# Moving the norm, the transposes, the logits and the choice of experts of seven token groups between the shared experts' slots

## The chip, the cores and the metric

The kernel runs as one program on one core of a Trainium2 chip. The metric is the device time of one launch in microseconds; the kernel before takes 1272.83 us, the median of three runs (1271.46 to 1273.12).

## The reference

The input is 8 x 512 tokens of 256 numbers, fp32. Three layers are applied in a row, each on a layer norm of the current x: half a mixture-of-experts layer, an attention layer with landmark tokens and an iterated pseudo-inverse, and the mixture-of-experts layer again with the same weights.

```python
def _L0_ffn_ref(hidden_states, gate_w, shared_gate, shared_up, shared_down, r_gate, r_up, r_down):
    x = hidden_states.reshape(-1, h)
    shared_out = _swiglu(x, shared_gate, shared_up, shared_down)      # silu(x @ wg.T) * (x @ wu.T) @ wd.T
    logits = x @ gate_w.T                                             # 8 experts
    top_id = jnp.argmax(logits, axis=-1)
    score = jax.nn.sigmoid(jnp.max(logits, axis=-1))
    xs = x * score[:, None]
    ... # for each expert e: routed += _swiglu(xs where top_id == e else 0, r_gate[e], r_up[e], r_down[e])
    return (shared_out + routed_out).reshape(b, s, h)

x = x + 0.5 * _L0_ffn_ref(_layernorm(x), ...)
x = x + _L0_attn_ref(_layernorm(x), ...)
x = x + 0.5 * _L0_ffn_ref(_layernorm(x), ...)
```

Every token goes to one expert only, and its row is scaled by the score before the expert's gate and up products.

## The kernel before

Everything is hand-scheduled: each engine (TensorE = PE, VectorE = DVE, ScalarE = ACT, GpSimd = POOL, SyncE = SP for DMAs) has one list of instructions that it works off in order, and semaphores make it wait for others. The 4096 tokens are 32 tiles of 128 rows, in 8 groups of 4 tiles. X stays in SBUF. A mixture-of-experts layer (the code calls it FFN, n = 0 and n = 1) has three stages.

The front stage, for every group g: DVE takes mean and variance (`bn_stats`, `bn_aggr`), ACT the square root (L897), DVE the reciprocal and the normalised rows (L364), PE transposes them with 8 matmuls against the identity (L1336), ACT copies the result from PSUM into XNT (L912). After groups 0 to 4 and again at the end PE makes the logits (L1363), ACT copies them (L916), PE turns them back (L1372), and DVE chooses the expert of every token (L452 to L460). Only then does PE start on the shared expert.

The shared expert is computed in 32 slots, slot = 4g + f, f being the quarter of the 512 hidden columns. In a slot PE does gate and up (L1403, 12 matmuls of 512 columns: a product of fp32 numbers is made from three products of their high and low parts), ACT the silu (L950), DVE the product h (L533), ACT its high part hh (L956), DVE its low part hl (L535), and PE the down product two slots later (L1416, 12 matmuls of 256 columns). Once in a group DVE adds the result onto X (`shared_out`, L527), ACT and DVE split the next group's transposed tokens (L935, L432). Beside it, in group 0, DVE counts the tokens of each expert and works out each token's slot in a table sorted by expert. POOL multiplies each row by norm and score (L1176 to L1182), SP stores it to `xs_dram` (L298), and POOL scatters the token numbers to `who_dram` (L1189), 4 tiles at a time. In slots 28 to 31 the first expert weights are split as well (ACT L966, DVE L557). They overwrite groups 0 to 5 of X, so ACT waits until these are stored (L305).

The routed stage has 39 tiles of the table. POOL gathers a tile's rows (L1202) and residual rows (L1208) and scatters the outcome (L1214); PE transposes the rows (`xt`, L1435), does gate and up (`through`, L1446), turns the hidden rows (L1453) and does down (L1460); ACT and DVE split rows and weights. For the first tile `xt` comes after all of the shared experts' work.

The attention stage between the two layers runs over periods, in which the steps of several batches are interleaved; the last period has only the output projection of the last batch left (`project`, L1682).

## Time and profile before

| what | us |
|---|---|
| median of three runs (lowest, highest) | 1272.83 (1271.46, 1273.12) |
| span of the profiled execution | 1266.7 |
| PE busy / DVE / ACT / POOL | 1143.0 / 768.9 / 601.1 / 582.6 |
| chain that ended last, PE's share | 73% |
| stage, FFN 0: until the first shared matmul | 0 to 44.4 |
| shared slots | 44.4 to 184.35 |
| routed tiles | 187 to about 398 |
| attention | about 400 to 887 |
| stage, FFN 1: front after attention | 887 to 912.7 |
| shared slots | 912.7 to 1051.4 |
| routed tiles | 1054 to 1266 |

No time of the profiled execution is given other than its span; the median lies 6.1 us above the span (start and end of the launch). PE is busy in nearly all of the shared and routed stages, and in the stages between them it is not.

### The profile page before, as it was taken

To read this page: it belongs to the slowest core of one execution; us is meant where nothing else is said; L and a number is where in the kernel's file an instruction comes from. 1 tells how busy PE (TensorE), PEld (TensorE's weight loads), DVE (VectorE), ACT (ScalarE), POOL (GpSimd) and SP (SyncE) were. 2 spreads that over 40 slices of the span, in tenths; PEclk is the share of its full clock that TensorE was granted. 3 is DMA by queue.
4 is the path that set the end of the run, shared out by engine and by line. 5 is a ranking of instruction groups with operands and counts; after the bars stand their busy time and mean duration, and the time that the engine had idled before them with its cause. 6 is when DMAs were issued, how large, how long until landed. Compare 5 with 4: busy or idle time off the path is not lost.

```text
span 1266.7 us, 29890 instructions
## 1 busy us (share of the span) xinstructions
PE 1143.0 (90%) x11140; PEld 933.2 (74%) x11141; DVE 768.9 (61%) x1467; ACT 601.1 (47%) x968; POOL 582.6 (46%) x624
## 2 busy tenths in 40 slices
PE   4899999999995689898898998986799998999997
PEld 2688877888884567667676776864588887888886
DVE  7554456666663574656757657652664455676664
ACT  2533336666663445445454543431533344666663
POOL 0388505767775121432423232232058713677675
PEclk9899999999997889999999999997799999999999
DMA  8311542222211200000000000000611343222220
GB/s 331 151 34 50 184 144 74 69 69 72 62 57 53 84 2 3 2 2 3 2 3 2 2 3 2 3 2 1 267 35 50 99 147 118 64 66 63 69 71 21
DMA packets 41964, 80.32 MB, mean 63 GB/s; under 512 B 8948, under 2 KB 33655, under 8 KB 40832
## 3 DMA queue, kind: packets, MB, share of 16 engines
q1 hardware_dynamic: 28576, 53.54, 11.7%
q0 software_dynamic: 13280, 25.24, 6.6%
q8 instruction: 80, 1.31, 0.4%
q14 instruction: 28, 0.23, 0.1%
HBM read 57.17 MB, written 27.07 MB: 67 GB/s over the span
## 4 chain that ended last, share of the span: by engine, by line
PE 73%; DVE 14%; ACT 6%; issue 5%; DMA 1%; POOL 0%; DVEq 0%; ACTq 0%; POOLq 0%
PE PS L1446 17%; PE PS L1403 11%; PE PS L1460 10%; PE PS L1416 6%; PE PS L1644 3%; PE PS L1631 3%; PE PS L1522 3%; PE PS L1453 3%; DVE A_NM L669 2%; PE PS L1682 2%; DVE A_NM L676 1%; PE PS L1532 1%; PE PS L1591 1%; PE PS L1435 1%; PE PS L1665 1%
## 5 line engine op out<-in xcount | busy, mean ns | idle before, releaser
L1446 PE MATMUL PS<-WHL,XGH 128*128 128x512 f32 x624 | 218.9, 432 | 8.2 <-DVE XGL L580 4.5
L1272 POOL TENSOR_TENSOR A_A<-A_XC,A_ST 128x320 f32<-128x320 f32 (+1 forms) x96 | 74.3, 789 | 193.5 <-ACT A_ST L1053 193.4
L1460 PE MATMUL PS<-WD,XNT 128*128 x624 | 148.4, 381 | 1.5 <-ACT XNT L989 1.5
L1202 POOL DMA_INDIRECT X<-xs_dram,WHO x78 | 117.7, 1508 | 48.8 <-issue 48.8
L587 DVE TENSOR_TENSOR XNT<-XNT,PS 128x512 f32<-128x512 f32 x78 | 53.6, 688 | 133.3 <-PE PS L1446 133.3
L1446 PEld LDWEIGHTS PS<-WHL,XGH 128*128 128x128 f32 x624 | 113.0, 192 | 28.2 <-DVE XGL L580 5.0
L1446 PE MATMUL PS<-WHL,XGL 128*128 128x512 f32 x312 | 124.5, 399 | 0.0
L1460 PEld LDWEIGHTS PS<-WD,XNT 128*128 128x128 f32 x624 | 112.5, 190 | 14.4 <-issue 2.0
L985 ACT ACTIVATE XNT<-PS 128x512 f32<-128x512 f32 x78 | 46.6, 598 | 150.4 <-PE PS L1446 150.4
L1208 POOL DMA_INDIRECT HSB<-shared_dram,WHO x78 | 80.2, 1028 | 79.6 <-DMA shared_dram<-X 56.4
L1416 PE MATMUL PS<-SDH,HHL 128*128 128x256 f32 x512 | 103.0, 285 | 2.3 <-DVE X L527 1.8
L557 DVE TENSOR_TENSOR WHL<-WG,WHL 128x1024 fp32r<-128x1024 f32 x78 | 94.7, 1215 | 2.6 <-ACT WHL L966 2.6
L557 DVE TENSOR_TENSOR WHL<-WU,WHL 128x1024 fp32r<-128x1024 f32 x78 | 95.1, 1219 | 0.0
L1416 PEld LDWEIGHTS PS<-SDH,HHL 128*128 128x128 f32 x512 | 83.7, 191 | 10.0 <-issue 7.7
L950 ACT ACTIVATE HSB<-PS 128x512 f32<-128x512 f32 x64 | 38.2, 597 | 107.3 <-PE PS L1403 106.8
L533 DVE TENSOR_TENSOR HSB<-HSB,PS 128x512 f32<-128x512 f32 x64 | 44.0, 688 | 64.8 <-ACT HSB L950 64.7
L1403 PE MATMUL PS<-XHL,SGH 128*128 128x512 f32 x256 | 82.0, 402 | 1.2 <-DVE XHL L432 1.2
L535 DVE TENSOR_TENSOR HHL<-HSB,HHL 128x512 fp32r<-128x512 f32 x64 | 48.4, 756 | 56.7 <-ACT HHL L956 56.7
L966 ACT CAST WHL<-WU 128x1024 fp32r x78 | 82.7, 1060 | 0.0
L966 ACT CAST WHL<-WG 128x1024 fp32r x78 | 81.8, 1048 | 1.7 <-issue 1.7
L1189 POOL DMA_INDIRECT who_dram<-STOK,SIDX x64 | 69.9, 1092 | 27.5 <-issue 14.3
L757 DVE SCALAR_TENSOR_TENSOR A_BU<-PS,A_XC 128x320 f32<-128x320 f32 (+1 forms) x96 | 41.1, 443 | 65.1 <-PE PS L1631 59.5
(240 smaller groups left out, 2700.4 us busy)
## 6 DMA issues: line engine op xcount, KB each, us to landing
WG<-in_r_gate SPq DMA_DIRECT2D x2, 4096.0 KB, 15.9
WU<-in_r_up SPq DMA_DIRECT2D x2, 4096.0 KB, 17.4
xs_dram<-X SPq DMA_DIRECT2D x16, 512.0 KB, 2.9
WD<-in_r_down SPq DMA_DIRECT2D x4, 2048.0 KB, 8.3
shared_dram<-X SPq DMA_DIRECT2D x16, 512.0 KB, 8.3
X<-in_x SPq DMA_DIRECT2D x4, 1024.0 KB, 9.0
X<-mid_dram SPq DMA_DIRECT2D x8, 512.0 KB, 3.8
X<-xs_dram,WHO POOLq DMA_INDIRECT x78, 3.6
```

What stands on the lines that cost most here:

```text
L535: dve.tensor_tensor(B["HHL"][2 * (f % 2) + 1][:], hidden, B["HHL"][2 * (f % 2)][:].bitcast(F32), ALU.subtract).then_inc(s["hl"], 1)
L557: dve.tensor_tensor(WHL[2 * slot + 1][:], B[w][:, bass.ds(ex * (KD * F), KD * F)], WHL[2 * slot][:].bitcast(F32), ALU.subtract).then_inc(s ...
L587: dve.tensor_tensor(B["RH"][:, u * F:(u + 1) * F], B["RS"][:, u * F:(u + 1) * F], banks[3 + u][:], ALU.mult).then_inc(s["rh"], 1)
L966: act.copy(WHL[2 * slot][:], B[w][:, bass.ds(ex * (KD * F), KD * F)]).then_inc(s["whi"], 1)
L1189: pool.indirect_dma_start(out=who_dram[n], out_offset=bass.IndirectOffsetOnAxis(ap=B["SIDX"][:, j:j + 1], axis=0), in_=B["STOK"][:, j:j + ...
L1202: pool.indirect_dma_start(out=B["XS"][:, u * D:(u + 1) * D], out_offset=None, in_=xs_dram, in_offset=bass.IndirectOffsetOnAxis(ap=B["WHO"] ...
L1208: pool.indirect_dma_start(out=B["RY"][:, u * D:(u + 1) * D], out_offset=None, in_=shared_dram, in_offset=bass.IndirectOffsetOnAxis(ap=B["W ...
L1272: pool.tensor_tensor(a, x, st, ALU.add).then_inc(att["a"], 1)
L1403: ins = pe.matmul(banks[bank][:], w[:, part], tok[:, k * GW:(k + 1) * GW], start=(k == 0 and i == 0), stop=(k == KD - 1 and i == 2))
L1416: ins = pe.matmul(to, h[:, j * P:(j + 1) * P], w[:, part], start=(f == 0 and i == 0 and j % 2 == 0), stop=(f == KF - 1 and i == 2), skip_g ...
L1446: ins = pe.matmul(banks[bank][:], tok, w[:, k * F:(k + 1) * F], start=(k == 0 and i == 0), stop=(k == KD - 1 and i == 2))
L1460: ins = pe.matmul(banks[7][:, 0:D], B["HT"][:, u * F + f * P:u * F + (f + 1) * P], B["WD"][:, bass.ds(ex * (KF * D) + f * D, D)], start=(f ...
```

## The change

The front stage is cut down to group 0. Groups 1 to 7 have their norm on POOL (`rows`, into WG's buffer that the routed weights fill later), their transposes on PE behind the gate and up product of slots 1, 2, 3, 6, 7, 8 and 9 (`TURN_SLOT`), and their copies on ACT. Logits come in slots 4 and 10, are turned in slot 11, the choice follows in slot 11 on DVE, and the counting and the slot table in slots 13 to 15. The square roots are done in four lots in FFN 0 and in two in FFN 1. Group 0's high and low token parts are taken straight from PSUM.

For FFN 1, group 0's square root, normalised rows, transposes and split stand in the last period of the attention stage.

The input loads are by group, with the shared weights between them. Rows are stored to `xs_dram` normalised but without the score. The score is written beside the token number into the slot table (8 bytes for each slot instead of 4), comes back with it, and is applied in the routed stage: as `scale` of ACT's silu, and as a factor of DVE's product of silu and up. The 32 scatters to `who_dram` are issued in one go after slot 14.

At the seam to the routed stage, `xt` of tile 0 stands in slot 31 and of tile 1 ahead of tile 0's gate product, the last two down products lie between tile 0's gate and up products, and in all routed tiles `xt` and the gather run one tile further ahead.

```diff
+    DEVIATIONS = [[(0, 1), (1, 2), (2, 4), (4, NG)], [(0, NG - 1), (NG - 1, NG)]]
+    TURN_SLOT = {1: 1, 2: 2, 3: 3, 4: 6, 5: 7, 6: 8, 7: 9}
+    LOGIT_SLOTS = (4, 10)
+    TURN_LOGITS_SLOT = 11
+    COUNT_SLOT = 13
...
@@ SP, loads
+        load_x(0)
+        sp.dma_start(CB[:], consts).then_inc(s_const, 16)
+        sp.dma_start(SG, sh_gate).then_inc(s_shared[0], 16)
+        load_x(1)
+        sp.dma_start(SU, sh_up).then_inc(s_shared[1], 16)
...
@@ SP, in ffn_dma
-            with sp.Fori(0, NG) as g:
-                need(sp, "xs", g * GT + GT)
-                sp.dma_start(xs_rows[:, bass.ds(g * GT, GT), :], B["XS"].rearrange("p (t d) -> p t d", d=D)).then_inc(s["xs_out"], 16)
+            for g in range(1, NG):
+                store_rows(g)
...
             need(sp, "who", 16 * NT)
             sp.dma_start(B["WHO"][:], who_dram[n].rearrange("(p t) o -> p (t o)", p=P)).then_inc(s["who_sb"], 16)
+            for g in range(PARTS_G - 1, NG - 1):
+                store(g)
@@ DVE
+                    if n == 0 and slot == 1:
+                        rstd(n, 2)
+                    if n == 0 and slot < NG - 3:
+                        dve.wait_ge(s_x[slot + 3], 16)
+                        stats(slot + 3, n)
+                    if slot == TURN_LOGITS_SLOT:
+                        choose()
+                    elif slot == COUNT_SLOT:
+                        count_tokens()
+                    elif slot == COUNT_SLOT + 1:
+                        count_tiles()
+                        find_slots()
...
-                dve.tensor_tensor(B["RH"][:, u * F:(u + 1) * F], B["RS"][:, u * F:(u + 1) * F], banks[3 + u][:],
-                                  ALU.mult).then_inc(s["rh"], 1)
+                dve.scalar_tensor_tensor(B["RH"][:, u * F:(u + 1) * F], banks[3 + u][:], score(t), B["RS"][:, u * F:(u + 1) * F],
+                                         ALU.mult, ALU.mult).then_inc(s["rh"], 1)
...
@@ DVE, last period of attention
+                if b == PERIODS[-1]:
+                    rstd(1, 0)
+                    wait_alone(att["num"], count("num", NG - 1, 2))
+                    first_rows(1)
...
@@ ACT, shared_group
+                    if slot in turns:
+                        tokens_kept(n, turns[slot])
+                    if slot in LOGIT_SLOTS:
+                        turned_logits(LOGIT_SLOTS.index(slot))
+                    if n == 0 and slot == 0:
+                        deviation(n, 2)
+                    if n == 0 and slot == NG - 4:
+                        deviation(n, 3)
+                    if slot == TURN_LOGITS_SLOT + 1:
+                        score()
...
-            ex = [expert(u) for u in range(2)]
+            ex = [expert(u) for u in range(UNR + 2)]
...
@@ POOL
+            def rows(g):
+                need("rstd", deviation_of(n, g) + 1)
+                if g > 4:
+                    need("xt_ready", g - 3)
+                    need("xs_out", 16 * (g - 3))
+                for j in range(GT):
+                    at = g * GT + j
+                    pool.tensor_scalar(xn_of(n, g)[:, j * D:(j + 1) * D], X[:, at * D:(at + 1) * D], MV[:, at * 2:at * 2 + 1],
+                                       RSTD[:, at:at + 1], ALU.subtract, ALU.mult).then_inc(s["xn"], 1)
...
+            for t in range(NT):
+                pool.indirect_dma_start(out=who_dram[n], out_offset=bass.IndirectOffsetOnAxis(ap=B["SLOT"][:, t:t + 1], axis=0),
+                                        in_=B["TOK"][:, t * 2:t * 2 + 2], in_offset=None).then_inc(s["who"], 16)
@@ PE, slots
+            for slot in range(KF * NG):
+                gate_up(slot // KF, slot % KF)
+                if slot in turns:
+                    g = turns[slot]
+                    need(pe, "xn", g * GT)
+                    need(pe, "xl0", KD)
+                    need(pe, "xt_sb", g * KD)
+                    if slot > LOGIT_SLOTS[0]:
+                        need(pe, "lgt_sb", 1)
+                    turn_rows_of(n, g)
+                if slot in LOGIT_SLOTS:
+                    logits(LOGIT_SLOTS.index(slot))
+                if slot == TURN_LOGITS_SLOT:
+                    turn_logits(0)
+                    turn_logits(1)
+                if slot == COUNT_SLOT:
+                    count_experts()
+                if slot == KF * NG - 1:
+                    need(pe, "silu", slot)
+                    xt(0, 0)
+                if slot >= 2:
+                    shared_down((slot - 2) // KF, (slot - 2) % KF)
@@ PE, tile_tensor
+                if first:
+                    xt(0, 1)
+                else:
                     need(pe, "rsilu", t)
                 through(1 + u % 2, t, u, 0, s["rg"])
-                if not first:
+                if first:
+                    for slot in (KF * NG - 2, KF * NG - 1):
+                        shared_down(slot // KF, slot % KF)
+                else:
                     ht(t - 1, (u - 1) % UNR)
...
                 if not last:
-                    xt(it if u < UNR - 1 else it + 1, (u + 1) % UNR)
+                    need(pe, "xgl", t + 2)
+                    xt(it + (u + 2) // UNR, (u + 2) % UNR)
@@ PE, last period of attention
+                if b == PERIODS[-1]:
+                    pe.wait_ge(att["ot"], count("ot", NG - 1, 2))
+                    first_turn(1)
```

PE's list at the start of the program, before (CB holds the identity, HB the normalised rows, GWT the gate's weights, SGH and SGL the shared gate weights' parts, XHL the tokens' parts):

```order
L1336 MATMUL PS<-CB,HB 128x128 x40
L1363 MATMUL PS<-XNT,GWT 32x512 x8
L1336 MATMUL PS<-CB,HB 128x128 x24
L1372 MATMUL PS<-CB,WD 128x4x8 x4
L1363 MATMUL PS<-XNT,GWT 32x512 x8
L1372 MATMUL PS<-CB,WD 128x4x8 x4
L1403 MATMUL PS<-XHL_0,SGH 128x512 x2
L1403 MATMUL PS<-XHL_0,SGL 128x512
```

The same place now (L1370 are the transposes, L1429 gate and up; rows of groups 1 to 7 lie in WG):

```order
L1370 MATMUL PS<-CB,X 128x128 x8
L1429 MATMUL PS<-XHL_0,SGH 128x512 x2
L1429 MATMUL PS<-XHL_0,SGL 128x512
```

and the end of slot 1 in it:

```order
L1429 MATMUL PS<-XHL_0,SUH 128x512 x2
L1429 MATMUL PS<-XHL_0,SUL 128x512
L1370 MATMUL PS<-CB,WG 128x128 x8
L1429 MATMUL PS<-XHL_0,SGH 128x512 x2
L1429 MATMUL PS<-XHL_0,SGL 128x512
```

Of the 64 transposes 8 are left ahead of the first slot; eight more stand behind slot 1's up product.

PE's list at the seam from the shared to the routed stage of FFN 0, before (L1416 is down, L1435 `xt`, L1446 the routed gate and up):

```order
L1416 MATMUL PS<-SDH,HHL_0 128x256
L1435 MATMUL PS<-CB,X 128x128 x2
L1430 TENSOR_LOAD EXPERT
L1430 ISA x2
L1430 TENSOR_LOAD EXPERT
L1430 ISA x2
L1446 MATMUL PS<-WHL,XGH 128x512 x2
L1446 MATMUL PS<-WHL,XGL 128x512
```

and now (L1444, L1451 and L1490 are the same three):

```order
L1444 MATMUL PS<-SDH,HHL_0 128x256
L1480 TENSOR_LOAD EXPERT
L1480 ISA x2
L1480 TENSOR_LOAD EXPERT
L1480 ISA x2
L1451 MATMUL PS<-CB,X 128x128 x2
L1490 MATMUL PS<-WHL,XGH 128x512 x2
L1490 MATMUL PS<-WHL,XGL 128x512
L1490 MATMUL PS<-WHL,XGH 128x512 x2
L1490 MATMUL PS<-WHL,XGL 128x512
L1444 MATMUL PS<-SDH,HHL_0 128x256
L1444 MATMUL PS<-SDL,HHL_0 128x256
```

The last two down products (24 matmuls) have moved behind the first routed gate product, and the `xt` in the piece is tile 1's.

POOL's list at the start of FFN 0, before (the split of the shared weights, the scaled rows, the scatter):

```order
L1170 TENSOR_TENSOR SGL<-WU,SGH 128x1024
L1170 TENSOR_TENSOR SUL<-WU,SUH 128x1024
L1170 TENSOR_TENSOR SDL<-WU,SDH 128x1024
L1176 COPY X<-X 128x1024
L1177 COPY RS_0<-RSC 128x4
L1178 COPY NM_0<-NMR 128x4
L1182 TENSOR_SCALAR X<-X,RS_0,NM_0 128x256 x4
L1185 COPY SIDX<-SLOT 128x4
L1186 COPY STOK<-TOK 128x4
L1189 DMA who_dram<-STOK,SIDX 4992x1 x4
```

and now:

```order
L1202 TENSOR_TENSOR SGL<-WU,SGH 128x1024
L1202 TENSOR_TENSOR SUL<-WU,SUH 128x1024
L1211 TENSOR_SCALAR WG<-X,MV,RSTD 128x256 x4
L1202 TENSOR_TENSOR SDL<-WU,SDH 128x1024
L1211 TENSOR_SCALAR WG<-X,MV,RSTD 128x256 x24
L1229 DMA who_dram<-TOK,SLOT 4992x2 x32
```

The 28 rows' instructions now stand ahead of all 32 scatters instead of between them.

## Rows read from the trace of the kernel before

**Rows 1.** Busy time by stage: stretch, its length, busy us (instructions) per engine, granted clock
```profile
44.40:184.35 139.95, 138.27 (x774) 119.49 (x775) 74.61 (x121) 49.50 (x76) 73.02 (x107) 0.99 0.32 110
...
192.80:388.00 195.20, 193.88 (x966) 160.74 (x967) 135.32 (x186) 122.84 (x185) 133.49 (x108) 1.00 0.20 62
...
873.00:912.70 39.70, 25.14 (x148) 17.96 (x142) 20.09 (x65) 15.67 (x31) 2.48 (x2) 0.70 0.52 213
```

**Rows 2.** Timeline, start of FFN 0, all engines: start, duration, instruction, idle before
```profile
6.30 1.41 DVE L378 BATCH_NORM_STATS2 STATS<-X 128x6 f32<-128x256 f32 x4 [5.31 <-DMA X<-in_x]
...
8.63 1.28 ACT L897 ACT_TABLE_LOAD   x1 [8.48 <-DVE MV L387]
9.93 0.30 ACT L897 ACTIVATE RSTD<-MV,CB 128x4 f32<-128x4 f32 x1
...
10.81 1.35 DVE L364 TENSOR_SCALAR HB<-X,MV,RSTD 128x256 f32<-128x256 f32 x4
...
12.31 1.94 PE L1336 MATMUL PS<-CB,HB 128*128 128x128 f32 x8 [12.31 <-DVE HB L364]
...
34.53 2.36 POOL L1170 TENSOR_TENSOR SGL<-WU,SGH 128x1024 fp32r<-128x1024 f32 x1 [34.06 <-ACT SGH L931]
```

**Rows 3.** Timeline of PE, matmuls in a warm stretch
```profile
50.20 0.62 PE L1403 MATMUL PS<-XHL,SGH 128*128 128x512 f32 x2
50.66 0.39 PE L1403 MATMUL PS<-XHL,SGL 128*128 128x512 f32 x1
...
889.11 1.09 PE L1336 MATMUL PS<-CB,HB 128*128 128x128 f32 x8 [2.53 <-DVE HB L364]
...
900.65 1.95 PE L1363 MATMUL PS<-XNT,GWT 128*32 128x512 f32 x16
```

**Rows 4.** Timeline of ACT, silu of slots 12 (both layers), 24 and 25
```profile
98.64 0.60 ACT L950 ACTIVATE HSB<-PS 128x512 f32<-128x512 f32 x1 [2.07 <-PE PS L1403]
...
965.91 0.60 ACT L950 ACTIVATE HSB<-PS 128x512 f32<-128x512 f32 x1 [2.07 <-PE PS L1403]
...
1016.89 0.60 ACT L950 ACTIVATE HSB<-PS 128x512 f32<-128x512 f32 x1 [2.07 <-PE PS L1403]
...
1021.07 0.60 ACT L950 ACTIVATE HSB<-PS 128x512 f32<-128x512 f32 x1 [2.07 <-PE PS L1403]
```

**Rows 5.** Timeline at the end of attention, three engines
```profile
878.83 0.67 ACT L897 ACTIVATE RSTD<-MV,CB 128x4 f32<-128x4 f32 x3
...
879.83 0.55 PE L1682 MATMUL PS<-A_WOH,A_OTH 128*128 128x256 f32 x1 [6.52 <-POOL A_OTL L1293]
...
886.62 0.69 DVE L798 TENSOR_TENSOR X<-PS,X 128x512 f32<-128x512 f32 x1 [3.09 <-PE PS L1682]
```

**Rows 6.** Timeline at the seam of FFN 0, DVE and PE
```profile
184.55 1.29 DVE L527 SCALAR_TENSOR_TENSOR X<-PS,X 128x512 f32<-128x512 f32 x2 [1.79 <-PE PS L1416]
...
186.98 0.90 PE L1446 MATMUL PS<-WHL,XGH 128*128 128x512 f32 x2 [2.25 <-DVE XGL L580]
...
190.66 0.70 PE L1446 MATMUL PS<-WHL,XGH 128*128 128x512 f32 x2
...
192.82 0.70 PE L1446 MATMUL PS<-WHL,XGH 128*128 128x512 f32 x2 [1.01 <-issue]
```

**Rows 7.** Instructions of two POOL lines (ns min/median/max), SP's store of group 5, ACT
```profile
L1182 POOL TENSOR_SCALAR X<-X,RS,NM x64: 545/550/2033, 49.0 to 1005.5; 128x256 f32<-128x256 f32 x64
...
L1189 POOL DMA_INDIRECT who_dram<-STOK,SIDX x64: 965/1003/1877, 64.4 to 1011.0; - x64
...
157.85 17.89 SPq L305 DMA_DIRECT2D shared_dram<-X  x2
...
165.48 1.05 ACT L966 CAST WHL<-WG 128x1024 fp32r x1 [0.95 <-issue]
```

**Rows 8.** Timeline of DVE, beside POOL's split at 39.16, and in a routed tile
```profile
39.39 3.20 DVE L432 TENSOR_TENSOR XHL<-XNT,XHL 128x1024 fp32r<-128x1024 f32 x1 [5.48 <-ACT XHL L935]
...
285.64 0.69 DVE L587 TENSOR_TENSOR XNT<-XNT,PS 128x512 f32<-128x512 f32 x1 [1.72 <-PE PS L1446]
```

450 lines of the change are left out of this document (215 added, 235 removed).

## The prediction, made before the changed kernel ran

> **What bounds the kernel now.** I read the busy time by stage first. In the shared slots of FFN 0 PE is busy 138.27 of 139.95 us, and a warm slot takes 1021.07 - 1016.89 = 4.18 us [rows 1, 4]: PE is the limit there. The front stages are different. PE's first matmul comes at 12.31, its first shared product at 44.40, and before FFN 1's slots PE is busy 25.14 of 39.70 us at a mean granted clock of 0.70 [rows 1, 2]. So I read the timeline of those stretches for what PE waits for, then the seam to the routed stage, where PE waits 2.25 us, runs cold until 190.66 and waits another 1.01 us [rows 6]. The change can win what PE idles or runs at half clock in these places, and pays with the front's PE work, which now lengthens the slots.
>
> **Prices of PE's work, warm.** Two matmuls of 512 columns start 50.66 - 50.20 = 0.46 us apart, so 0.23 each: gate and up of a slot 12 x 0.23 = 2.76. Down is the rest of 4.18, 1.42. Eight transposes last 1.09 with a tail of about 0.13, so 0.96; one half of the logits 1.95, 1.85 without the tail [rows 3, 4]. Turning the logits back is taken as another 0.96. Cold, the nine matmuls from 186.98 to 190.66 take 0.41 each on average and eight transposes 1.94 [rows 2, 6]; I take 0.43 for a fully cold one. The granted clock is half (1.2 GHz) there. Moved into the slots of each layer: 7 x 0.96 + 2 x 1.85 + 0.96 = 11.4 us.
>
> **FFN 0, start.** Today 1 MB of X is issued first and used at 6.30. Half of that at the roughly 0.34 MB/us of the first 30 us saves 1.5, so group 0 starts at 4.8. Today statistics and their copy take from 6.30 to 8.63, of which 0.3 goes with the copy; then root 0.30, a reciprocal (0.2) and rows 1.35 [rows 2], about 8.6; transposes cold 1.94: 10.6. ACT meanwhile splits the gate weights (landed about 7.5) and the up weights (10.6, done 11.6), then group 0's high parts, 0.62 each; DVE's low part 0.69: first product at 13.0. POOL's splits of 2.36 each [rows 2] end at 11.0 and 14.1, ahead of the up product at 15.6. Slot 0 cold, 12 x 0.43 = 5.2: 18.2. Slot 1 with its transposes and slot 2's gate and up, warm, 2.76 + 0.96 + 2.76: 24.6.
>
> There PE waits. Group 2's root is in a lot with group 3, whose statistics DVE takes only after slot 0's low part: silu 18.4, h, hh and hl of 0.6 to 0.7 each (21.0), stats 1.8 (22.7), root 0.3, a table load back to silu 1.28 (24.2), slot 1's silu, h, hh and hl, behind which the reciprocal is queued on DVE (27.0), and POOL's four rows of 0.55 [rows 7] (29.2). PE idles 4.6 us. It will be cold for the next 3.7 us as after the 2.25 us wait of rows 6, costing 1.8.
>
> From 29.2 to slot 12: six transposes 5.8, logits 3.7, turned 0.96, nine gate and ups 24.8, ten downs 14.3, one wait for `shared_out` 0.7: 50.3, and 1.8 for the clock: 81.3. Today slot 12's silu starts at 98.64 [rows 4], so its gate at 98.64 - 2.92 = 95.7. That is 14.4 less. Taken back: counting in slot 13 instead of slot 0, 0.5, and about 0.9 because DVE's counting, slot table and `shared_out` now fall in three slots in a row (some 14.6 us of work in 12.6). Net 13.0.
>
> **FFN 1, start.** ACT's first root at 878.83 [rows 5] stays, all seven groups in one. Reciprocal and rows end at 880.8, the eight cold transposes at 882.8. The projection that starts at 879.83 today goes behind them and so 3 us later: 885.4, DVE's addition 886.2, group 0's low parts 887.4, second projection 889. PE goes straight on into slot 0 at 888.9, where DVE's last addition was at 886.62 and the slots began at 912.7 [rows 1, 5]. Slot 0 cold 5.2, then 11 x 2.76 + 10 x 1.42 + 11.4 = 56.0: slot 12's gate at 950.2. POOL's rows come every 2.2 us from 890.2, faster than slots use them. Today it is 965.91 - 2.92 = 963.0. Less 1.4 as above: net 11.4.
>
> **Seams.** Counted from the end of slot 31's up product, the second tile starts 13.1 us later today (179.7 to 192.82) [rows 6]. Now: tile 0's transposes 0.24, down 1.42, tile 1's 0.24, gate 1.38, two downs 2.84, up 1.38, 0.24, and a wait of 0.3 for `shared_out` (1.29, after the last down): 8.1. The two row splits lie under the downs. So 5.0 a layer, 10.0. I take 1.0 back, as the residual rows still need the store of group 7 and one gather, and DVE's first `tile_out` stands before the weight split of tile 3. Five register loads instead of two before the weight splits of ACT and DVE: 0.5 for both layers.
>
> **Sum.** 13.0 + 11.4 + 10.0 - 1.0 - 0.5 = 32.9 us. The span of 1266.7 becomes 1233.8; with the 6.1 us by which the median of the runs shown, 1272.83, stands above it, 1239.9; so 1240.
>
> **Edits at nothing, and their bounds.** The score in the routed stage: one factor more on an instruction of 0.69, idle 1.72 before it [rows 8]; a form with one factor more (`shared_out`) takes 1.29 for two [rows 6], so 0; its slack up to PE's use of the up weights is 1.3 us a tile, beyond which each 0.1 costs 7.8. The run-ahead of `xt`: PE is busy 193.88 of 195.20 us in the routed tiles [rows 1], so between 0 and a gain of 1.3 a layer, about 3 in all; I take 0. ACT's extra copies and table loads, 2.9 us at the score in slot 12, lie in the 4 us between a silu and the gate that needs its h. Stores and weight loads move earlier on SP; nobody waits for them but POOL and, at the seam, ACT (third rival).
>
> **A rule on the table loads.** In the trace the load is followed by the root 1.30 us after its start (8.63 to 9.93) [rows 2]. The Trainium skill (ScalarE: Activation LUTs, What ACT_TABLE_LOAD costs) puts a switch at about 1.28 for the load and 1.38 for a drain, 2.66 in all. No such drain is seen here. By the rule the wait at slot 2 would be 1.4 longer and the time 1241.3; by the row it is 1239.9, which stays.
>
> **A rule on POOL beside DVE.** DVE's low part of the tokens took 3.20 beside POOL's split [rows 8], and is held up nowhere else so long. The 28 rows and three splits of POOL now fall beside DVE's work, the splits from 8.6 to 19.2. The Trainium skill (SBUF — State Buffer, SBUF: two separate sides) has DVE instructions with two SBUF inputs and POOL's exclude each other for a whole instruction. If it holds, all 28 rows cost DVE 28 x 0.55 = 15 us a layer at the worst, and with its slack gone that would end near the first rival's time below. Today 32 such rows of 0.55 and eight copies lie in the slots too, and PE hardly waits there [rows 1, 7], so I add nothing.
>
> **Rivals.**
> 1. More waits in the early slots. The chain ACT, DVE, POOL, PE of FFN 0 has a dozen hops that I priced with few gaps, and slots 1 to 9 have each a wait for rows, for the copy before and for PSUM. For it: PE is busy 98.8% of today's slots with less queued on ACT and DVE [rows 1]. Against: a silu has about 4 us until the gate that needs its h (a down, a gate and up and a down lie between). A mean of 0.7 us in 18 slots is 12.6 us: 1252.5. Chance 0.14.
> 2. The run-ahead wins too: 3 us, and the wait in slot 2 is half of mine (another 3): 1234. Chance 0.05.
> 3. The slot table comes late. Scatters start after slot 14 (about 99) instead of 63, then 32 in a row of 1.00 + 0.30 us: 141, landed at 144; the table is read back, and only behind it SP stores group 5 (157.85 today) [rows 7], which ACT waits for before the weight splits, 165.48 today [rows 7] and about 150 now. The slack is some 2 us. From there each us is lost in both layers. The point at which the gain is gone is (32.9 / 2 + 2) / 32 = 0.58 us more for a scatter, 1.88 with its gap. If one with 8 bytes took the longest of today's, 1.88 and 0.30 of gap, the 32 take 70 us instead of 42, 26 late in each layer after the slack: 1240 + 52 = 1292. For it: nothing is between them now that lets the queue empty. Against: four in a row today keep 1.3. Chance 0.06.
> 4. The work only changes places: PE's idle time comes back as cold clock and waits, 1273. For it, PE's busy sum of 1143 us hardly moves. Against, that sum counts cold matmuls twice as long. Chance 0.02.
>
> **How the numbers follow.** Forecast 0.73, rivals 0.14, 0.05, 0.06, 0.02. The forecast's own range is 1233 to 1248. With the better part of the first rival and the second the range is 1231 to 1254, which leaves out the third and fourth, the tail of the first and some of the forecast's own error. Within 0.2% (2.5 us, what a measurement of this kernel can tell from none) falls the fourth, 0.02; slower is the third, 0.06; faster the rest, 0.92.
>
> **What would show it.** The first shared product at about 13 and 889; a wait of PE of about 4.6 us behind slot 2 of FFN 0 and none above 1 in FFN 1; slot 12's silu near 84 and 953; the seam's second tile 8 us after slot 31; routed tiles of 5.2 as before; ACT at the weight splits not waiting for the store of group 5. It is wrong if the slots 3 to 11 take more than 5.6 us each on average, if DVE's product in the routed tiles takes over 2 us, or if the wait for the slot table shows on PE.

## The result

The changed kernel takes 1315.18 us (median of six runs, 1312.04 to 1324.49), the kernel before in the same session 1272.97: ratio 1.036, interval 1.0328 to 1.0392. It is slower by 42 us, where 33 less were forecast. The profiled execution has a span of 1322.4, one of the longer ones.

First the account, from the starts of ACT's silu in the timelines of both kernels. A layer is cut at the silu of slots 12 and 31 and of the second and the last routed tile.

| from, to | before | after | difference | forecast |
|---|---|---|---|---|
| start, slot 12 of FFN 0 | 98.64 | 94.25 | -4.4 | -14.4 |
| slots 12 to 31 | 81.28 | 111.31 | +30.0 | +1.4 |
| slot 31, second tile | 14.57 | 9.43 | -5.1 | -5.0 |
| second tile, last tile | 194.32 | 198.32 | +4.0 | +0.8 |
| attention, until POOL's last split | 488.28 | 500.13 | +11.9 | 0 |
| from there to slot 12 of FFN 1 | 88.82 | 75.84 | -13.0 | -12.8 |
| slots 12 to 31 | 81.06 | 112.38 | +31.3 | +1.4 |
| slot 31, second tile | 14.57 | 9.43 | -5.1 | -5.0 |
| second tile, last tile | 193.42 | 199.35 | +5.9 | +0.8 |
| last tile, end | 11.74 | 11.96 | +0.2 | 0 |

The rows add up to the 55.7 between the two profiled spans. The attention stage has a shorter and a longer form in kernels with the same attention code (last section), and these two profiles have one of each. Without its 11.9, 43.8 is left, near the 42 of the medians. In the column of the forecast the 1.0 for the residual rows and the 0.5 for register loads stand with the routed tiles, half in each layer.

Busy time by stretch after the change (columns as in [rows 1]):

```profile
13.84:125.39 111.55, 100.35 (x554) 83.70 (x555) 57.42 (x134) 47.41 (x74) 46.43 (x38) 0.94 0.47 168
125.39:162.05 36.66, 16.71 (x72) 12.06 (x70) 4.26 (x7) 4.50 (x7) 22.64 (x24) 0.68 0.04 6
...
925.00:1010.00 85.00, 82.90 (x495) 68.47 (x494) 40.06 (x81) 35.87 (x58) 38.64 (x30) 1.00 0.45 162
1010.00:1060.00 50.00, 29.75 (x124) 22.23 (x123) 11.68 (x19) 8.51 (x13) 29.69 (x31) 0.73 0.21 64
```

In both layers one stretch stands out, in which PE, DVE and ACT hardly work and POOL goes on; in FFN 0 the DMA engines are idle too (share 0.04). The stretch from 1010 to 1060 takes in some slots without a stall and so looks milder. It is the row of 32 scatters. The timeline in it, all engines:

```profile
134.67 0.28 PE L1444 MATMUL PS<-SDH,HHL 128*128 128x256 f32 x1
135.12 0.96 POOL L1229 DMA_INDIRECT who_dram<-TOK,SLOT  x1 [0.30 <-issue]
135.98 0.28 PE L1444 MATMUL PS<-SDH,HHL 128*128 128x256 f32 x1 [1.03 <-issue]
...
139.51 0.58 PE L1429 MATMUL PS<-XHL,SGH 128*128 128x512 f32 x1 [1.02 <-issue]
...
142.35 0.59 PE L1429 MATMUL PS<-XHL,SGH 128*128 128x512 f32 x1 [1.40 <-issue]
...
143.83 0.62 ACT L974 CAST HHL<-HSB 128x512 fp32r<-128x512 f32 x1 [9.36 <-remote]
...
154.08 0.96 POOL L1229 DMA_INDIRECT who_dram<-TOK,SLOT  x1 [0.30 <-issue]
159.23 0.60 ACT L968 ACTIVATE HSB<-PS 128x512 f32<-128x512 f32 x1 [14.78 <-remote]
...
163.56 0.50 SPq L340 DMA_DIRECT2D WHO<-who_dram  x1
```

The matmuls come one by one, inside a product that waits for nobody. Their idle time is put down to "issue" (the profile shows nothing that the engine waited for), ACT's to "remote" (a signal whose sender the profile does not name). ACT's silu at 159.23 starts 6 us after the product that it needs. The scatters themselves are as fast as priced (0.96 and 0.30 of gap). The first was issued at 113.6, not at 99 as rival 3 had it.

The other rows that answer to those of before: ACT's silu of slot 12 in both layers [rows 4], PE's wait for group 2's rows, the seam [rows 6], and POOL's rows [rows 7] (ns min/median/max).

```profile
94.25 0.60 ACT L968 ACTIVATE HSB<-PS 128x512 f32<-128x512 f32 x1 [2.12 <-PE PS L1429]
...
989.28 0.60 ACT L968 ACTIVATE HSB<-PS 128x512 f32<-128x512 f32 x1 [2.12 <-PE PS L1429]
```

```profile
13.84 1.19 PE L1429 MATMUL PS<-XHL,SGH 128*128 128x512 f32 x2 [1.49 <-DVE XHL L400]
...
34.68 1.97 PE L1370 MATMUL PS<-CB,WG 128*128 128x128 f32 x8 [8.80 <-POOL WG L1211]
```

```profile
209.15 0.69 ACT L1014 ACTIVATE XNT<-PS,WHO 128x512 f32<-128x512 f32 x1 [1.03 <-PE PS L1490]
...
214.99 0.69 ACT L1014 ACTIVATE XNT<-PS,WHO 128x512 f32<-128x512 f32 x1
```

```profile
L1211 POOL TENSOR_SCALAR WG<-X,MV,RSTD x56: 1211/1223/2585, 15.5 to 960.0; 128x256 f32<-128x256 f32 x56
```

POOL needs 1.22 us for a row, not 0.55, and PE waits 8.8 us in slot 2, where 4.6 were forecast.

### The profile page after: what moved, and what is told of

The parts are those of the page before. It is cut to its first block, busy times and chain, and to the rows that moved or that the text cites. A ratio compares the mean times of both kernels' runs of the same rounds, so it can differ in the third digit from the quotient of the medians.

```text
span 1322.4 us, 29548 instructions
## 1 busy us (share of the span) xinstructions
PE 1160.8 (88%) x11140; PEld 940.1 (71%) x11141; DVE 748.2 (57%) x1383; ACT 609.2 (46%) x967; POOL 562.0 (43%) x536
## 4 chain that ended last, share of the span: by engine, by line
PE 70%; DVE 12%; issue 7%; ACT 5%; POOL 2%; another core or an unknown queue 2%; DMA 1%; DVEq 1%; ACTq 0%; SPq 0%; POOLq 0%
PE PS L1490 14%; PE PS L1429 11%; PE PS L1504 9%; PE PS L1444 6%; PE PS L1693 3%; PE PS L1680 3%; PE PS L1571 3%; PE PS L1497 2%; DVE A_NM L670 2%; PE PS L1731 2%; POOL WG L1211 2%; PE PS L1451 1%; DVE A_NM L677 1%; PE PS L1581 1%
## 5 line engine op out<-in xcount | busy, mean ns | idle before, releaser
L1490 PE MATMUL PS<-WHL,XGH 128*128 128x512 f32 x624 | 216.9, 429 | 3.4 <-DVE WHL L556 3.3
L1234 POOL DMA_INDIRECT X<-xs_dram,WHO x78 | 102.0, 1307 | 120.7 <-PE PS L1451 67.8
L1490 PEld LDWEIGHTS PS<-WHL,XGH 128*128 128x128 f32 x624 | 111.3, 189 | 22.4 <-issue 2.7
L1444 PE MATMUL PS<-SDH,HHL 128*128 128x256 f32 x512 | 108.4, 294 | 21.2 <-DVE X L516 13.9
L584 DVE SCALAR_TENSOR_TENSOR XNT<-PS,WHO,XNT 128x512 f32<-128x512 f32 x78 | 58.3, 747 | 121.4 <-PE PS L1490 106.7
L1490 PE MATMUL PS<-WHL,XGL 128*128 128x512 f32 x312 | 123.1, 394 | 0.0
L1014 ACT ACTIVATE XNT<-PS,WHO 128x512 f32<-128x512 f32 x78 | 53.8, 690 | 147.3 <-PE PS L1490 134.1
L1444 PEld LDWEIGHTS PS<-SDH,HHL 128*128 128x128 f32 x512 | 86.7, 197 | 30.1 <-issue 28.5
L1229 POOL DMA_INDIRECT who_dram<-TOK,SLOT x64 | 62.8, 981 | 103.2 <-issue 103.2
L974 ACT CAST HHL<-HSB 128x512 fp32r<-128x512 f32 x64 | 39.7, 620 | 143.1 <-PE PS L1444 79.7
L1429 PE MATMUL PS<-XHL,SGH 128*128 128x512 f32 x256 | 84.6, 409 | 14.6 <-issue 11.9
L524 DVE TENSOR_TENSOR HSB<-HSB,PS 128x512 f32<-128x512 f32 x64 | 43.8, 684 | 85.4 <-ACT HSB L968 83.8
L1429 PE MATMUL PS<-XHL,SUH 128*128 128x512 f32 x256 | 83.7, 407 | 3.7 <-issue 3.7
L1211 POOL TENSOR_SCALAR WG<-X,MV,RSTD 128x256 f32<-128x256 f32 x56 | 72.2, 1305 | 33.7 <-DVE RSTD L386 24.5
L996 ACT CAST WHL<-WG 128x1024 fp32r x78 | 82.7, 1060 | 5.1 <-issue 5.1
```

Source lines behind the costliest of these rows:

```text
L584: dve.scalar_tensor_tensor(B["RH"][:, u * F:(u + 1) * F], banks[3 + u][:], score(t), B["RS"][:, u * F:(u + 1) * F], ALU.mult, ALU.mult).th ...
L996: act.copy(WHL[2 * slot][:], B[w][:, bass.ds(ex * (KD * F), KD * F)]).then_inc(s["whi"], 1)
L1211: pool.tensor_scalar(xn_of(n, g)[:, j * D:(j + 1) * D], X[:, at * D:(at + 1) * D], MV[:, at * 2:at * 2 + 1], RSTD[:, at:at + 1], ALU.subtr ...
L1229: pool.indirect_dma_start(out=who_dram[n], out_offset=bass.IndirectOffsetOnAxis(ap=B["SLOT"][:, t:t + 1], axis=0), in_=B["TOK"][:, t * 2:t ...
L1234: pool.indirect_dma_start(out=B["XS"][:, u * D:(u + 1) * D], out_offset=None, in_=xs_dram, in_offset=bass.IndirectOffsetOnAxis(ap=B["WHO"] ...
L1429: ins = pe.matmul(banks[bank][:], w[:, part], tok[:, k * GW:(k + 1) * GW], start=(k == 0 and i == 0), stop=(k == KD - 1 and i == 2))
```

## The experiments

The table has every timed run of the whole kernel. e1, e2 and e5 each start from the changed kernel, e4 from the kernel before. e6 joins e5's waits and e2's rows; e7, e8, e10 and e13 each add one edit to the one before in this list. e9 starts from e7, e11, e12 and e17 from e8, e18 and e19 from e17. The ratio is to the kernel before in the same session, whose median was between 1264 and 1271 us; medians of different sessions differ by some us for that reason alone.

"Slots" is the time from the silu of slot 12 to that of slot 27 in FFN 0 and FFN 1, read in each run's timeline: 63.78 in both layers before, 65.2 by the forecast (63.78 and the 1.4 of the count), 91.84 and 92.87 after.

| run | median us | ratio to before (interval) | slots |
|---|---|---|---|
| e1_paced | 1288.47 | 1.0168 (1.0149, 1.0187) | 65.20, 65.20 |
| e2_multadd | 1306.09 | 1.0296 (1.0269, 1.0323) | 90.83, 90.62 |
| e4_burst | 1323.62 | 1.0451 (1.0412, 1.0491) | 89.65, 89.34 |
| e5_pace8 | 1268.81 | 0.9997 (0.9964, 1.0029) | 68.24, 65.87 |
| e6_pace8_multadd | 1256.19 | 0.9905 (0.9869, 0.9941) | 66.26, 66.02 |
| e7_two_loads | 1259.57 | 0.9910 (0.9876, 0.9945) | 66.57, 66.11 |
| e8_run_ahead | 1256.17 | 0.9894 (0.9832, 0.9956) | 66.60, 68.29 |
| e9_pace4 | 1263.85 | 0.9947 (0.9911, 0.9984) | 65.24, 65.22 |
| e10_turns | 1254.78 | 0.9852 (0.9787, 0.9918) | 66.46, 67.40 |
| e11_never_empty | 1306.74 | 1.0287 (1.0224, 1.0349) | 92.87, 92.56 |
| e12_pace16 | 1302.17 | 1.0222 (1.0143, 1.0302) | 88.85, 90.78 |
| e13_pace6_4 | 1243.41 | 0.9800 (0.9766, 0.9834) | 65.28, 65.21 |
| e17_sp_quiet | 1250.18 | 0.9899 (0.9834, 0.9963) | 65.24, 65.20 |
| e18_load_only | 1249.86 | 0.9889 (0.9830, 0.9948) | 65.27, 65.20 |
| e19_stores_only | 1243.59 | 0.9803 (0.9751, 0.9855) | 65.24, 65.19 |

### The row of scatters

```diff
 e1 (e5 and e9 alike, with 8 and 4, and the store of group 5 ahead of the read of the table)
             for t in range(NT):
+                if t and t % 4 == 0:
+                    need("who", 16 * t)
                 pool.indirect_dma_start(out=who_dram[n], ...)
```

> The changed kernel, with POOL waiting after every four scatters until all issued so far have landed, as before the change. Theory A (32 scatters in flight hold up the engines' instruction supply and every other DMA): PE's runs of single matmuls with idle time put down to issue, about 29 us in FFN 0 and 30 us in FFN 1, are gone. But the table is then complete only after 8 x (4 x 1.27 + 2.3) = 59 us, near 173, and store 5 stands behind the read of the table, so ACT's weight splits wait some 10 to 15 us in each layer: 1315 - 59 + 25, about 1280. Theory B (eight bytes a slot or the late table cost the time, not their number in flight): the idle issue time stays and the wait for the table is added, 1330 or more.

1288.5, and PE, idle for 20 us of this stretch after the change, is busy all of it:

```profile
125.39:162.05 36.66, 36.66 (x210) 31.38 (x209) 17.15 (x24) 12.55 (x20) 21.50 (x23) 1.00 0.07 19
```

What is left is the late table: the step from slot 27 to 28 takes 22.1 and 22.7 us instead of 7.5, behind the store of group 5. So the row without waits is what costs the time, as theory A has it; whether it is the number in flight comes with e11.

```diff
 e4, on the kernel before
-            seated(0)
             with pool.Fori(1, NG) as g:
                 scored(g)
-                need("who", g * (16 * GT))
-                seated(g)
+            for t in range(NT):
+                pool.indirect_dma_start(out=who_dram[n], ... in_=B["TOK"][:, t:t + 1])
```

> The kernel before, with its 32 scatters of 4 bytes a slot in a row behind all the scaled rows, straight from the slot table, nothing else changed. They start near 105 in FFN 0 and end near 146, long before the table is used at 187. Theory A (the number in flight is the cause): PE stalls here too, single matmuls with idle issue time, 15 to 30 us a layer, 1300 to 1330. Theory B (the table's lateness or its 8 bytes): nothing, 1273 within 3.

1323.6, 56 more than before. The stall comes along with the row, with 4 bytes a slot and a table that nobody waits for. So neither the eight bytes nor the lateness is the cause.

> The changed kernel, with a wait for landing after every eight scatters and the store of group 5 ahead of the read of the table. Theory A, if eight in flight are few enough: the stalls are gone, the table is complete after 4 x (8 x 1.27 + 2.3) = 50 us, near 163, and nobody waits for it: 1315 - 59, about 1256. If eight are already too many: stalls of some us for each eight, 1270 to 1290. Theory B: 1315 or more.

1268.8, 12 above theory A's number. The stalls are nearly gone, and the slots fell by 50.6 us in both layers together, where theory A took off 59. The other 4 lie within the spread between runs.

```diff
 e11, batches of four, each waiting for the one two before it
+                odd = t // 4 % 2
+                landed = "who_odd" if odd else "who"
+                if t >= 8 and t % 4 == 0:
+                    need(landed, 64 * (t // 8))
```

> The run with the run-ahead of one tile, with the 32 scatters in batches of four on two counters in turn: a batch waits for the landing of the batch two before it. So never more than eight are in flight, as in the run it starts from, but the queue is not drained between the batches. Theory F (an engine that needs new instructions gets them only when the queue of scatters is empty): stalls as in the changed kernel, 20 to 30 us a layer, 1296 to 1310. Theory G (the number in flight, or the backlog, sets it): no stall beyond the 2 to 4 us with eight, and the table 5 us earlier, 1253 to 1257.

1306.7 and 93 us for the slots. Never more than eight are in flight, as in e5, but the row is unbroken, and it stalls. So the number in flight is not the cause.

> The run with the run-ahead of one tile, with one wait for landing after 16 scatters instead of one after every eight. An engine that needs instructions would wait for the rest of a batch: a batch of eight lasts 12 us and cost 2 to 4 us a layer, one of 16 lasts 24 us and should cost 8 to 15 us a layer, 1272 to 1286. Rival: only the backlog late in a row of 32 matters, 1256 to 1260.

1302.2: two rows of 16 cost 24 to 26 us a layer, far more than the 8 to 15 expected, and nearly as much as one of 32. Lengths of 4, 8, 16 and 32 cost 0, 1 to 3, 24 to 26 and 25 to 28 us a layer. Most of it falls into the second row: in FFN 0 PE is busy 19.74 of 23.00 us in the first and 7.62 of 22.20 in the second. There the stall has another form. PE does not idle inside its product; DVE has the product h ready at 140.93, ACT starts the high part that waits for it at 150.30, and PE waits for that chain:

```profile
140.24 0.69 DVE L534 TENSOR_TENSOR HSB<-HSB,PS 128x512 f32<-128x512 f32 x1 [3.58 <-ACT HSB L980]
...
150.30 0.62 ACT L986 CAST HHL<-HSB 128x512 fp32r<-128x512 f32 x1 [10.09 <-remote]
...
152.99 0.55 PE L1460 MATMUL PS<-SDH,HHL 128*128 128x256 f32 x1 [14.58 <-DVE X L525]
```

### What the row holds up

Between 134 and 153 us of the changed kernel's trace PE starts most instructions, weight loads too, 0.70 us or a multiple after one before; some come in pairs closer than that. I first took this for a starved supply of instructions. Two small programs, with the row of scatters but none of SP's transfers beside it:

> A small program that computes nothing of the reference (it copies x to the output), to measure the disputed effect by itself. Two parts, each with 32 scatters in a row of 8 bytes a slot. In part 1 PE runs 700 matmuls of 512 columns written out one by one and ACT 560 small copies in a loop of 28; in part 2 PE runs its 700 in a loop of 28 and ACT its 560 written out. No engine waits for another within a part. Theory H (a row of scatters holds up the supply of new instructions): PE starts late in part 1 once what it has loaded is used up, part 1 of PE takes 161 us and 20 or more on top, ACT's loop goes on; in part 2 PE's loop takes 161 and ACT's written-out copies stall. Theory S (the row holds up the signals between engines): nobody stalls in either part. Theory B (it slows the engines or their memory as such): both forms slow down alike.

> The same small program with a wait for landing after every four scatters. Theory H: the written-out lists stall for less than 3 us in all, since every gap between two batches lets the supply through; PE takes about 161 us in both parts. Theories S and B as before: no difference between the two programs but POOL's time.

Spans of 361.4 and 362.1: no stall in either, in written-out lists or loops. So a row by itself does not hold up the supply, and theory H falls as it stands. As nothing stalls in these programs, they cannot tell what is held up in the kernel, where something does.

The Trainium skill (Runtime: NRT & Kernel Launch, Instruction fetch mechanics) says that the cost of going from one fetched block of instructions to the next is mostly hidden. m14 agrees: PE is busy 160.45 of 161.00 us while it works through its written-out list.

> The small program again (it computes nothing of the reference), with the 32 scatters in a row, now to addresses 312 bytes apart from partition to partition as in the slot table instead of side by side, and with a third part in which PE, ACT and DVE work as in the shared slots: 28 groups of 24 matmuls written out, ACT waits for PE, DVE for ACT, PE for DVE, with a row of 32 scatters beside groups 4 to 12. Theory H is out, since written-out lists went on at full speed. Theory A (spread addresses): all three parts stall now. Theory S (signals between the engines): only part 3 stalls, by 20 us or more over its 154. If no part stalls, it takes something else of the kernel.

Its three parts, PE busy throughout:

```profile
4.00:160.00 156.00, 155.05 (x671) 128.12 (x672) 0.79 (x4) 61.20 (x562) 30.79 (x32) 1.00 0.09 26
165.00:225.00 60.00, 60.00 (x266) 49.68 (x266) 0.00 (x0) 58.17 (x550) 26.32 (x28) 1.00 0.02 1
340.00:500.00 160.00, 160.00 (x707) 132.51 (x706) 18.54 (x27) 15.85 (x27) 30.64 (x32) 1.00 0.01 1
```

No part stalls. In this program the row alone does nothing to the other engines, with spread addresses and with signals between the engines. What the kernel has beside it are SP's transfers:

```diff
 e17, on e8 without its pacing; e18 puts the load of WD back ahead of the wait, e19 the stores
             store(1)
-            need(sp, "expert_of", 1)
-            sp.dma_start(B["WD"][:, half:], r_down[:, half:]).then_inc(s["wd"], 16)
-            for g in range(2, PARTS_G):
-                store(g)
             need(sp, "who", 16 * NT)
             sp.dma_start(B["WHO"][:], ...).then_inc(s["who_sb"], 16)
+            need(sp, "expert_of", 1)
+            for g in range(2, PARTS_G):
+                store(g)
+            sp.dma_start(B["WD"][:, half:], r_down[:, half:]).then_inc(s["wd"], 16)
```

> The run with the run-ahead of one tile, with the 32 scatters in a row again, and SP issuing nothing beside them: the load of half the down weights and the stores of groups 2 to 5 stand behind the read of the table. Theory Q (the row stalls the engines only together with SP's large transfers or its waiting store): no stall of the slots, but the stores come late, near 160, 1256 to 1265. Rival (the row alone): stalls as before, slots 12 to 27 at 89 to 93 us in each layer, 1305 or more.

1250.2: 32 scatters in a row, no stall. With the late stores the step from slot 27 to 28 takes 11.0 and 10.5 us, 5 more in each layer than in e19 below (5.9 and 5.6).

> The run with SP quiet, with the load of 2 MB (half the down weights) ahead of the wait for the table again, so beside the row of 32 scatters; the stores stay behind. Theory L (the load, which holds the DMA engines for some 8 us at the start of the row and lets scatters pile up, sets off the stall): stalls as in the changed kernel, slots 12 to 27 at 89 to 93 us, 1300 or more. Theory T (the stores, or SP's wait for a group's result between them, do it): no stall, 65 us, about 1250.

> The run with SP quiet, with the stores of groups 2 to 5 ahead of the wait for the table again, so beside the row; the load of 2 MB stays behind it. Theory L: no stall, slots 12 to 27 at 65 us a layer, and as ACT no longer waits for stores before its weight splits, 5 us a layer less than with SP quiet, about 1242. Theory T: stalls, 1300 or more.

Neither stalls; both expectations had one of them do it. PE in the row, e11 (stalled), e19 and e18:

```profile
120.00:150.00 30.00, 15.08 (x60) 10.58 (x59) 2.27 (x4) 1.81 (x3) 22.03 (x23) 0.69 0.02 2
```

```profile
106.00:150.00 44.00, 43.53 (x247) 37.04 (x245) 22.89 (x39) 15.83 (x25) 32.39 (x32) 1.00 0.09 26
```

```profile
106.00:150.00 44.00, 43.53 (x248) 37.11 (x247) 22.68 (x39) 16.06 (x25) 32.70 (x32) 1.00 0.15 49
```

So, as far as these runs show, it takes three things together: an unbroken row of 16 or more, the 2 MB load at its start, and the 512 KB stores behind that load. No run has all three on the very kernel of e18 and e19; the nearest are e11 and e12, in which the waits in POOL's list differ as well. Whether it is their presence beside the row or their order in SP's list that matters was not separated either.

In FFN 0 after the change SP's queue moves nothing after 128 and PE's first gap is at 134.9, so it is not their bandwidth. From 134 to 150 only two queues move anything, POOL's scatters (q0) and one block of instructions on q14:

```profile
q0 software_dynamic: 416, 0.01, 2.1%
q14 instruction: 1, 0.01, 0.2%
```

Blocks of instructions of 16 KB come on q8, one each 18 to 28 us in the slots of the kernel before. The last one ahead of the stall was read from 127.67 to 128.55, 6 us before the first gap, and the next came only at 176.3, so a block that is late does not explain the gap either. Both forms of the stall, PE's slow issue and ACT's late start behind a finished product (e12), are seen; what in the hardware is held up, the supply of instructions past the fetch, the signals between the engines or both, stays open.

### POOL's rows

```diff
-                    pool.tensor_scalar(..., MV[:, at * 2:at * 2 + 1], RSTD[:, at:at + 1], ALU.subtract, ALU.mult)
+                    pool.tensor_scalar(..., RSTD[:, at:at + 1], MV[:, at * 2:at * 2 + 1], ALU.mult, ALU.add)
```

> The changed kernel, with POOL's 28 rows a layer written as row x rstd + (-mean x rstd) (mult, add) in place of (row - mean) x rstd (subtract, mult); DVE works out -mean x rstd in one small instruction more for each lot of square roots. Theory A (the pair of operations sets POOL's duration): rows fall from 1.22 to 0.55 us as in the kernel before, PE's waits for rows in slots 1 to 9 of FFN 0 (12.9 us in the trace) shrink by 6 to 9 us, little in FFN 1: 1306 to 1309. Theory B (the buffer written or DVE at work beside it sets it): rows stay at 1.22 and the time within 2 us of 1315.

1306.1, 9 less by the medians of two sessions, 8 by the ratios (1.0296 after 1.036). POOL's rows and DVE's (ns min/median/max):

```profile
L1214 POOL TENSOR_SCALAR WG<-X,RSTD,MV x56: 555/562/2042, 18.8 to 944.5; 128x256 f32<-128x256 f32 x56
```

```profile
L395 DVE TENSOR_SCALAR X<-X,RSTD,MV x8: 402/408/2546, 7.6 to 907.7; 128x256 f32<-128x256 f32 x8
```

The same buffers, the same neighbours, 0.56 instead of 1.22: the pair of operations sets it. (On DVE it makes no difference: 0.41 us a row with either.) But in this run the four first rows on DVE, 0.3 us later than after the change while POOL's split came 0.6 earlier, met that split, and took 5.61 instead of 1.38:

```profile
7.59 5.61 DVE L395 TENSOR_SCALAR X<-X,RSTD,MV 128x256 f32<-128x256 f32 x4 [0.16 <-DVE MV L388]
```

```profile
7.92 2.34 POOL L1205 TENSOR_TENSOR SGL<-WU,SGH 128x1024 fp32r<-128x1024 f32 x1 [7.46 <-ACT SGH L932]
```

The Trainium skill (SBUF — State Buffer, SBUF: two separate sides) states such an exclusion: a DVE instruction in a mode with two ports, and one of POOL, hold the ports that they share for a whole instruction, and the other waits. If this row is in such a mode, the trace agrees: the two of the four rows that start together with a split last 2.49 and 2.55 us, the splits 2.34 each.

> The changed kernel with a wait for landing after every eight scatters, the store of group 5 ahead of the read of the table, and POOL's rows of groups 1 to 7 as mult, add; group 0's rows on DVE stay subtract, mult, and DVE works out -mean x rstd only for groups 1 to 7. Theory: the two gains add up. From 1268.8 with the pace alone, 9 less as for the pair of operations alone, and 2 less because DVE's first rows are ahead of POOL's first split again (1.38 instead of 5.61 for the four): 1258. Rival: PE's waits for rows were covered by the stalls, or the waits move to ACT's and DVE's chain, 1265 or more.

1256.2 (expected 1258). With group 0 kept as it was, slot 12 of FFN 0 comes at 87.56 instead of 94.83 in e5.

```diff
 e10
-    TURN_SLOT = {1: 1, 2: 2, 3: 3, 4: 6, 5: 7, 6: 8, 7: 9}
-    LOGIT_SLOTS = (4, 10)
+    TURN_SLOT = {1: 1, 2: 3, 3: 4, 4: 6, 5: 7, 6: 8, 7: 9}
+    LOGIT_SLOTS = (5, 10)
```

> The run with the run-ahead of one tile (eight scatters between waits), with group 2 turned in slot 3 and group 3 in slot 4 instead of 2 and 3, and the first logits in slot 5 instead of 4. Theory: PE's wait for POOL's rows of group 2 behind slot 2 of FFN 0 (slots 2 to 3 take 8.9 us where 5.1 is PE's work) goes, and with it the cold stretch behind it: 4 to 5 us less in FFN 0, nothing in FFN 1, 1251. Rival: the next link of the chain (the silu, the product, group 3's copy) waits as long, no gain.

Slot 12 of FFN 0 at 82.50 against 86.99, as expected (and 82.27 in e13; with the old order it comes between 87.0 and 89.0 in e6 to e9, e11, e12 and e17 to e19). The median is only 1.4 lower, the ratio 0.0042, some 5 us, with wide intervals; the profiled run of e10 has the long attention stage, that of e8 the short one.

### The seam and the routed tiles

```diff
 e7, ACT in slot 28
-            ex = [expert(u) for u in range(UNR + 2)]
+            ex = [expert(u) for u in range(2)]
```

> As the run before in this list, and ACT loads two expert numbers instead of five ahead of its weight splits in slot 28, the other three behind the seam. Theory: ACT's idle issue time of 2.52 there falls to about 1.0 and the step from slot 27 to 28 from 7.6 to 6.0 in each layer, 3.3 less in all: 1255. Rival: the loads come back in the first routed tile, where PE waits for ACT's splits: no gain.

ACT ahead of its first weight split in FFN 1, after the change and in e7:

```profile
1086.80 1.05 ACT L996 CAST WHL<-WG 128x1024 fp32r x1 [2.57 <-issue]
```

```profile
1027.83 1.05 ACT L1008 CAST WHL<-WG 128x1024 fp32r x1 [0.71 <-issue]
```

Slot 27 to 28 takes 5.7 instead of 7.6 there: 1.9 a layer. The median does not show it (1259.6 against 1256.2, overlapping intervals; its profiled run has the long attention stage, 517.5 against 504.7).

```diff
 e8, PE (ACT's and DVE's parts alike)
-                if not last:
-                    need(pe, "xgl", t + 2)
-                    xt(it + (u + 2) // UNR, (u + 2) % UNR)
+                if not last and not first:
+                    xt(it if u < UNR - 1 else it + 1, (u + 1) % UNR)
```

> As the run before in this list, and from the second routed tile on the transposes of a tile's rows run one tile ahead as in the kernel before, not two; the seam stays as changed. Theory C (the longer run-ahead puts register arithmetic and a wait ahead of PE's transposes in every third tile, the gap of 0.3 us put down to issue): tiles 4 to 35 fall from 5.28 to 5.34 us each to 5.20, 2 to 4.5 us a layer, so about 1249. Rival D (the score as scale of the silu and factor of the product costs it): no change, 1255.

From the second to the last tile 194.82 and 196.64 instead of 197.83 and 198.37 in e7: 3.0 and 1.7. This pair alone would be weak, as e10 and e12, with the routed tiles of e8, took 197.91 and 198.28 in FFN 0. Over all runs it holds: with a run-ahead of two no run came under 196.6 in FFN 0 and 198.4 in FFN 1, with one e13, e17, e18 and e19 all took 193.7 or 193.8, and 194.9 (the former runs are all from earlier sessions). Theory C is supported; as to rival D, the score is still in these tiles. The gap in every third tile after the change, PE and its weight loads:

```profile
271.33 0.40 PE L1490 MATMUL PS<-WHL,XGL 128*128 128x512 f32 x1
271.81 0.20 PEld L1451 LDWEIGHTS PS<-CB,X 128*128 128x128 f32 x2 [0.52 <-issue]
271.84 0.41 PE L1451 MATMUL PS<-CB,X 128*128 128x128 f32 x2
```

> As the run with two loads, with a wait after every four scatters instead of eight. If eight in flight still hold PE up (slots 22 to 24 of FFN 0 took 5.1, 5.7 and 5.9 instead of 4.2 and 4.5 with eight), 3 us less. Against it the table is complete some 10 us later, near 173, with its read at 176 and the first gather behind it, needed in slot 31 near 180: a wait of 0 to 4 us a layer. I expect 1253 to 1260.

1263.9, above the expected range. The slots are clean, but in FFN 0 the table is 8.5 us late at the seam (17.92 instead of 9.43):

```profile
181.09 0.66 PE L1466 MATMUL PS<-CB,X 128*128 128x128 f32 x2 [5.69 <-DMA X<-xs_dram,WHO]
```

> The run with group 2 turned in slot 3, with waits after every six scatters in FFN 0 and after every four in FFN 1, where a batch of four cost nothing and the table came in time. Theory F (only an unbroken row of scatters starves the engines): slots 12 to 27 fall from 66.46 to 65.5 and from 67.40 to 65.2 us, and the step from slot 27 to 31 of FFN 0 from 19.63 to about 18; against that the table of FFN 0 comes 5 us later, which should still be in time or cost up to 2. Together 2 to 4 us less, 1251 against 1254.8. A difference as small as this lies within the spread of the attention stage (some 10 us between runs), so the slots are what is read.

1243.4, better than expected; the ratio is 2.0% below the kernel before (1.7 to 2.3). With e19, which needs no waits at all, it is the fastest measured. e19 still turns group 2 in slot 2 and reaches slot 12 at 88.80, where e13 comes at 82.27; the two edits were not run together. PE waits 1.12 us for group 2's rows:

```profile
31.31 1.09 PE L1386 MATMUL PS<-CB,WG 128*128 128x128 f32 x8 [1.12 <-POOL WG L1225]
```

## Why the prediction was wrong

- **The row of scatters.** The step that failed is the one that lets the row run beside the slots for nothing. The sum has no term for it, and rival 3 saw it only as a late table ("nothing is between them now that lets the queue empty"), priced by its own length, with a chance of 0.06 and a threshold of 1.88 us a scatter. SP's load and stores beside it were put at nothing as well ("nobody waits for them but POOL and, at the seam, ACT"). But a scatter kept its 1.26, and nobody waited for the table first; PE, ACT and DVE stood still beside it. It measured 27 us a layer (92 and 93 against 65.2), 54 in all. That rival 3's 1292 lies on the side of the measured 1315 is no merit of its mechanism. No row of before showed more than four in a row, so the unknown had no bound above, and should have had one.
- **POOL's rows, 0.55 each.** The row I took was a `mult, add`, the new one a `subtract, mult`: 1.22. It cost 7.3 us at the start of FFN 0 (e5 to e6) and about 2 in FFN 1. The wait of 4.6 in slot 2 became 8.8, and with rows of 0.56 it is 5.3 (e6, e8). The prediction's fear of DVE and POOL excluding each other is not what made the rows long: beside the same work they take 0.56 as `mult, add`.
- **The wait at slot 2 itself.** I took it as given. Turning the group a slot later removes it, 4.5 us (e8 to e10).
- **Five register loads, 0.5 for both layers.** They cost 1.9 a layer, as they stand ahead of the splits for which PE waits (e7).
- **The run-ahead of `xt`, 0 to a gain of 3.** It cost 3.0 and 1.7 (e7 to e8), some 3 us a layer by all runs.
- **Right.** First product at 13.84 (13.0). The start of FFN 1, -13.0 (-12.8), with rows at 1.22 and slots nonetheless in time. The seam, -5.1 (-5.0). The slots with count and table, 65.2. Slots with transposes 5.1. The score as a factor cost nothing that shows: the tiles 4 to 35 take 160.7 and 161.9 in e19, 161.4 and 161.2 before.
- **The table loads.** After the change the load at 97.90 lasts 1.28 and the silu follows at 99.19; no drain shows, and the sum by the row stands.
- **The 6.1 us on top of the span.** They are not the start and end of the launch. Where both are known the time stands 1.8 to 2.1 us above the span of the same execution (1324.49 and 1322.4); the other 4 say that the profiled execution of before was shorter than the three timed ones.
- **The sum.** e13, with these steps put right, takes 1243.4. That this is near the 1239.9 forecast is partly luck: the kernel before took 1265.8 in its session, so the gain is 22.4 us and not 33, and 4.5 of it come from turning groups 2 and 3 later, which was not forecast. By the stages of its profile e13 is 35.3 us shorter than before outside of attention (32.9 were forecast for the same stages) and 12.7 longer in attention, where the forecast had 0. So most terms of the sum were about right, some errors cancelled, and the large loss came from a term that it did not have.

## What to carry to other kernels

A row of the same small DMA that was never issued unbroken before is a new resource use: look for a bound on what it does to the other engines, and not only on how long it takes. Here a wait for landing after every four or six, or moving the large load away from its start, took the loss away. Take a duration only from a row with the same pair of operations. When engines idle on "issue" inside a product, look for what another queue does at that time, not for a semaphore.

## What the runs showed of the hardware

- An unbroken row of 16 or 32 scatters beside a 2 MB load and the stores behind it costs 24 to 28 us a layer. PE starts most instructions 0.70 us or a multiple apart, or waits for ACT and DVE, which start up to 9 us after what they wait for is done; POOL keeps its 1.26 us a scatter. Without the load (e19), without the stores (e18) or with waits after every four (e1, e9) the slots take the 65.2 us of no stall; with waits after every eight 0.7 to 3.1 more.
- POOL: 128 x 256 fp32 with two per-partition scalars takes 1.22 us as `subtract, mult` and 0.56 as `mult, add`.
- DVE's row of 0.41 takes up to 2.55 when it starts with POOL's split of 2.34 (e2).
- The attention stage has two lengths in kernels with the same attention code. From the last routed silu of FFN 0 to FFN 1's slot 0 it takes 503.5 in e8 and 517.65 in e10. In the long one PE's granted clock falls below full for a while, as after the change:

```profile
644.00:704.00 60.00, 55.22 (x931) 41.90 (x930) 36.80 (x85) 26.84 (x46) 18.02 (x22) 0.93 0.01 2
```

This is the spread of 10 us within each kernel's runs, and why the small steps were read in the slots and not in the medians. Why one run has the long form and another the short one stays open, and so does whether the change makes the long one more frequent: the profiled runs of the kernel before and of e4 have the short one, those of the changed kernel and of eight of the fourteen variants built on it the long one.
